# Routed slots of a two-layer kernel: who fetches a slot's rows and who turns them

## The reference

```
x  = x + attn0(xn) + ffn0(xn)        # chunked linear attention; 16 gated experts of width 128, all tokens
xn = layernorm(x)
x  = x + attn1(xn) + ffn1(xn)
attn1: top-2 of 4 gated linear scans  h_t = a_t*h_{t-1} + sigmoid(g)*tanh(v)
ffn1:  logits = xn @ gate_w.T + gate_b + expert_bias;  e = argmax(logits)     # one of 8 experts a token
       y = relu(xn @ w1[e] + b1[e]) @ w2[e] + b2[e]                           # 256 -> 1024 -> 256
```

## Time and profile before

| what | us |
|---|---|
| runs of the kernel before | 1044.45 median (1044.31 to 1044.87, 3 runs) |
| the profiled execution | 1045.66 |
| its span | 1043.9 |
| TensorE busy | 1032.9 (99% of the span) |
| VectorE busy | 769.4 (74%) |
| ScalarE busy | 629.2 (60%) |
| GpSimd busy | 318.4 (31%) |

### The profile page before, as it was taken

One profiled execution on the slowest core, in us unless ns is written; L12 is line 12 of the kernel. 1 busy time (PEld: TensorE's weight loads), 2 busy tenths in 40 slices (PEclk: granted clock), 3 DMA queues, 4 the chain that ended last, 5 costly groups with the idle time before them and its releaser, 6 DMA issues. The chain is left out here.

```text
span 1043.9 us, 19992 instructions
## 1 busy us (share of the span) xinstructions
PE 1032.9 (99%) x6566; PEld 921.3 (88%) x6566; DVE 769.4 (74%) x1247; ACT 629.2 (60%) x1186; POOL 318.4 (31%) x284
## 2 busy tenths in 40 slices
PE   8999999999999999999999999999999999999998
PEld 7988888889888888888877888999999999888887
DVE  6876667666666666767779998877777677588887
ACT  4654445444444454545566666788888888566665
POOL 3343343443434344343452782000000000372000
PEclk9999999999999999999999999999999999999999
DMA  6135213022131221623156275587887776552203
GB/s 195 60 97 202 82 41 100 6 79 55 40 100 40 80 60 41 217 67 142 42 202 262 82 268 205 183 269 266 275 273 252 266 253 212 210 170 90 84 17 102
DMA packets 108402, 148.46 MB, mean 142 GB/s; under 512 B 39616, under 2 KB 76352, under 8 KB 107328
## 3 DMA queue, kind: packets, MB, share of 16 engines
q1 hardware_dynamic: 99584, 133.80, 38.7%
q0 software_dynamic: 3072, 8.39, 2.4%
q10 hardware_dynamic: 5696, 5.64, 1.6%
HBM read 105.53 MB, written 42.27 MB: 142 GB/s over the span
## 5 line engine op out<-in xcount | busy, mean ns | idle before, releaser
L793 POOL TENSOR_TENSOR acc<-acc,ytmp 128x512 f32<-128x512 f32 x120 | 156.4, 1303 | 260.2 <-ACT ytmp L884 240.0
L1602 ACT ACTIVATE act_o<-ps,scan_bias 128x512 f32<-128x512 f32 x189 | 129.7, 688 | 100.0 <-PE ps L392 95.8
L884 ACT ACTIVATE ytmp<-ps,sel 128x256 f32<-128x256 f32 x256 | 107.3, 470 | 99.4 <-PE ps L1141 98.7
L961 DVE SCALAR_TENSOR_TENSOR hT_l<-ps,hT_h 128x512 fp32r<-128x512 f32 x128 | 87.8, 686 | 89.4 <-ACT hT_h L844 88.6
L1139 PE MATMUL ps<-vals_h,hT_h 128*128 128x256 f32 x512 | 145.3, 284 | 1.1 <-DVE hT_l L961 0.7
L1140 PE MATMUL ps<-vals_l,hT_h 128*128 128x256 f32 x512 | 143.6, 281 | 0.0
L1141 PE MATMUL ps<-vals_h,hT_l 128*128 128x256 f32 x512 | 143.5, 280 | 0.0
L844 ACT ACTIVATE hT_h<-ps 128x512 fp32r<-128x512 f32 x128 | 76.3, 596 | 96.5 <-PE ps L392 89.5
L1926 DVE TENSOR_TENSOR_SCAN h_b<-a_b,hstate,xs_b 128x512 f32<-128x512 f32 x63 | 88.2, 1400 | 30.3 <-ACT a_b L1609 26.8
L1754 POOL DMA_INDIRECT late_y<-y_d,pos_i x20 | 23.1, 1157 | 273.0 <-DMA y_d<-y_sb 267.2
L1139 PEld LDWEIGHTS ps<-vals_h,hT_h 128*128 128x128 f32 x512 | 96.3, 188 | 11.1 <-issue 4.6
(11 more groups left out here) (258 smaller groups left out, 2765.5 us busy)
## 6 DMA issues: line engine op xcount, KB each, us to landing
raw<-w SPq DMA_DIRECT2D x78, 512.0 KB, 4.3
x1T<-xT_d SPq DMA_DIRECT2D x16, 512.0 KB, 5.1
comb_b<-comb_d SPq DMA_DIRECT2D x8, 1024.0 KB, 8.3
xn_d<-xn SPq DMA_DIRECT2D x15, 512.0 KB, 2.9
w_small<-w SPq DMA_DIRECT2D x14, 512.0 KB, 4.3
xs_d<-zeros ACTq DMA_DIRECT2D x1, 4992.0 KB, 19.7
x_d<-x SPq DMA_DIRECT2D x8, 512.0 KB, 4.5
xT_d<-nT_h SPq DMA_DIRECT2D x8, 512.0 KB, 2.6
```

The costliest lines, as they stand in the source:

```text
L793: pool.tensor_tensor(dst[:, 2:4, :], acc[:, 2:4, :], ytmp[:, k % 2, :, :], ALU.add).then_inc(acc23, 1)
L884: act.activation(ytmp[:, k % 2, j - 2, :], yb(k, j), ACT.Copy, scale=sel[:, j, k:k + 1]).then_inc(y_23, 1)
L1602: act.activation(act_o[:, i % 2, w, :], ps[:, 3 * (i % 2) + w, :], func, bias=scan_bias[:, w, i:i + 1]).then_inc(act_g, 1)
```

## The change

- TensorE no longer turns rows. VectorE does it, with one transpose instruction per slot (`turn_rows`) that turns 32x32 squares. So that this gives the full transpose, the rows are laid out in SBUF in another way: partition quarter q holds columns 64q to 64q+63 of 32-row pieces, and the host permutes the rows of `w1` to match.
- The rows come in four transfers for a slot, one for each quarter, of 32 partitions and 256-byte runs, issued by GpSimd (`load_rows` on `pool`) once the transpose of the slot before them in the list is done (`turned`). Before it was one transfer on SyncE's queue, with 1 KB runs.
- In a plain slot VectorE turns the next rows after piece 0, ScalarE rounds them after piece 1 and VectorE makes their rest after piece 2. In a big slot VectorE turns after piece 2, and the other two stay at the end. `sT_small` is written by VectorE directly.
- In scan group 3 GpSimd makes the products of steps 4 to 7 and the sums of steps 6 and 7; both were VectorE's.
- SyncE loads the plain slot's weights at the end of its list for k = 0, behind the other weights.
- The rankings stand one behind each piece of slot 21; before, all stood at its end with `mixture_top`, which is now in slot 22.

The core of the diff:

```diff
-    rows = rc("rows", [P, ST, D], F32)
+    rows = rc("rows", [P, ST * P // Q32, DC * Q32], F32)
+    sT32 = rc("sT32", [P, DC, SLOT], F32)
-    xs_v = xs_d.rearrange("(b p) d -> b p d", p=P)
+    xs_q = xs_d.rearrange("(g r) (b k) -> b r g k", r=Q32, b=P // Q32)
...
+    def mixed_on_dve(g, i):
+        return isinstance(g, int) and g >= 2 and not (g == B_FIRST - 1 and i >= MC - DC)
+    def product_on_pool(g, i):
+        return zero(g) or (isinstance(g, int) and g == B_FIRST - 1 and i >= MC // 2)
...  SyncE, slot(r, k)
                 if left(r, k) > 1:
-                    load_rows(r, k + 2)
-                    if k == 0:
-                        load_w1_small(r, expert_at(r, ST))
...
                 if left(r, k) > 1:
                     raw2_half(n + 2, 0, expert_at(r, k + 2))
+                    if k == 0:
+                        load_w1_small(r, expert_at(r, ST))
...  TensorE
-            def rows_T(r, k):
-                pe.wait_ge(rows_in, 16 * (n + 1))
-                for c in range(DC):
-                    for i in range(st):
-                        last_mm = pe.transpose(ps[:, 6, (c * st + i) * P:(c * st + i + 1) * P],
-                                               rows[:, i, c * P:(c + 1) * P], ident[:])
-                if left(r, k) > 0:
-                    rows_T(r, k + 1)
...  ScalarE, slot(r, k)
                     relu(n, k, q, st * P)
                     round_e(n, q, st * P)
+                    if q == 1 and small(k):
+                        rows_hi(r, k + 1)
...
-                    rows_hi(r, k + 1)
+                    if not small(k) and not small(k + 1):
+                        rows_hi(r, k + 1)
...  GpSimd
+            def load_rows(r, k):
+                n = ROUND * r + k
+                if not zero(n):
+                    wait_alone(pool, turned, n)
+                b, st = blocks(r, k)
+                n_q = P // Q32
+                for q in range(n_q):
+                    quarter = slice(q * Q32, (q + 1) * Q32)
+                    pool.dma_start(rows[quarter, 0:st * n_q, :],
+                                   xs_q[q][:, bass.ds(b * n_q, st * n_q), :]).then_inc(rows_in, 16)
+            for g in range(B_FIRST - 1):
+                body(g)
+            all_scattered(pool)
+            load_rows(0, 0)
+            body(B_FIRST - 1)
+            every_slot(load_next, pool)
...  VectorE
+            def turn_rows(r, k):
+                n, (_, st) = ROUND * r + k, blocks(r, k)
+                dve.wait_ge(rows_in, 16 * (P // Q32) * (n + 1))
+                dst = sT_small if small(k) else sT32
+                if not small(k) and not zero(n):
+                    dve.wait_ge(sT_ok, bigs(r, k))
+                dve.transpose(dst[:].rearrange("p c (g r) -> p g c r", r=Q32),
+                              rows[:, 0:st * P // Q32, :].rearrange("p g (c a) -> p g c a", c=DC)).then_inc(turned, 1)
...  VectorE, slot(r, k)
                     low_e(n, q, st * P)
+                    if left(r, k) == 1:
+                        mixture_rank(dve, link, mix2, q)
+                    if q == (0 if small(k) else 2) and left(r, k) > 0:
+                        turn_rows(r, k + 1)
+                    if q == 2 and small(k):
+                        rows_lo(r, k + 1)
```

More of the change, by code:

```diff
@@ L51 @@
 CHUNK = 32
+Q32 = 32
 Q32 = 32
@@ L597, in build @@
     w1_hi, w1_lo, w2_hi, w2_lo = (sem(n) for n in ("w1_hi", "w1_lo", "w2_hi", "w2_lo"))
-    T_full, sT_hi, sT_ok = sem("T_full"), sem("sT_hi"), sem("sT_ok")
+    turned, sT_hi, sT_ok = sem("turned"), sem("sT_hi"), sem("sT_ok")
     l1_full, t_ok, e_hi, e_ok, l2_part, ys_ok, y_st = (
@@ L1344, in raw2_half @@
                              a["w2"][bass.ds(e, 1), h].rearrange("a p j d -> p (a j) d")).then_inc(r2_in[h], 16)
[L1346 to L1351, removed]
             def load_b1(n, k, e):
@@ L1528, in slot @@
                 W = st * P
-                pe.wait_ge(sT_ok, n + 1)
+                if small(k):
+                    pe.wait_ge(turned, n + 1)
+                else:
+                    pe.wait_ge(sT_ok, bigs(r, k) + 1)
                 for q in range(FJ // 2):
@@ L1626, in rows_hi @@
             def rows_hi(r, k):
[L1627 to L1633, removed]
+                act.wait_ge(turned, ROUND * r + k + 1)
+                act.activation(sT_h[:], sT32[:], ACT.Copy).then_inc(sT_hi, 1)
             def relu(n, k, q, W):
@@ L1716, in _, with xs @@
             pool.memset(within[:, :, 0:1], 0.0).then_inc(r_io, 1)
[L1718 to L1722, removed]
+            def xs(g, i):
+                n = MC * g + i
+                if n >= 2:
+                    pool.wait_ge(scan_ok, n - 1 if product_on_pool(g, i - 1) else n)
+                pool.wait_ge(act_g, 3 * n + 2)
                 pool.tensor_tensor(xs_b[:, i % 2, :], act_o[:, i % 2, 0, :], act_o[:, i % 2, 1, :],
@@ L1758, in body @@
                 if zero(g):
-                    xs(0)
+                    xs(g, 0)
                 for i in range(MC):
-                    if zero(g) and i + 1 < MC:
-                        xs(i + 1)
-                    if i >= DC and not mixed_on_dve(g):
+                    if i + 1 < MC and product_on_pool(g, i + 1):
+                        xs(g, i + 1)
+                    if i >= DC and not mixed_on_dve(g, i):
                         mix(g, i)
@@ L1768, in _, with load_next @@
             rstd(pool, mv1, stats1[:, :, 0], rstd1, mvs1, pe1, rs1, GROUPS - 1)
-            for g in range(B_FIRST):
+            def load_rows(r, k):
[8 more added lines that the diff above has]
+                                   xs_q[q][:, bass.ds(b * n_q, st * n_q), :]).then_inc(rows_in, 16)
+            def load_next(r, k):
+                if left(r, k) > 0:
+                    load_rows(r, k + 1)
+            for g in range(B_FIRST - 1):
                 body(g)
+            all_scattered(pool)
+            load_rows(0, 0)
+            body(B_FIRST - 1)
+            every_slot(load_next, pool)
             pool.wait_ge(y_st, 16 * NSLOT)
@@ L1912, in step @@
                     return
-                if not zero(g):
+                if not product_on_pool(g, i):
                     dve.wait_ge(act_g, 3 * n + 2)
@@ L1941, in step @@
                                   ALU.mult).then_inc(hw_ok, 1)
-                if i >= DC and mixed_on_dve(g) and not (final(g) and i >= MC - DC):
+                if i >= DC and mixed_on_dve(g, i) and not (final(g) and i >= MC - DC):
                     if i >= MC - DC:
@@ L2000, in rows_out @@
                                   ALU.add).then_inc(ys_ok, 1)
-            def mixture_pieces(slots_left):
-                if slots_left == 1:
-                    for j in range(M):
-                        mixture_rank(dve, link, mix2, j)
-                    mixture_top(dve, link, mix2)
-                else:
-                    mixture_finish(dve, link, mix2, 2)
             def slot(r, k):
@@ L2023, in slot @@
                 if left(r, k) > 0:
-                    if not small(k + 1):
+                    if not small(k) and not small(k + 1):
                         rows_lo(r, k + 1)
@@ L2028, in slot @@
                     w2_half(n + 1, 0)
-                if left(r, k) < 2:
-                    mixture_pieces(left(r, k))
+                if left(r, k) == 0:
+                    mixture_top(dve, link, mix2)
+                    mixture_finish(dve, link, mix2, 2)
             g = GROUPS - 1
@@ L2061, in _ @@
                         w1_half(0, (i - 4) // 2)
+                    if g == B_FIRST - 1 and i == MC - 4:
+                        turn_rows(0, 0)
                     if g == B_FIRST - 1 and i == MC - 3:
@@ L2098 @@
         "expert_bias": c(i["L1_ffn_expert_bias"]),
-        "w1": c(i["L1_ffn_w1"].reshape(E1, DC, P, 2, F1 // 2).transpose(0, 3, 2, 1, 4)),
+        "w1": c(i["L1_ffn_w1"].reshape(E1, P // Q32, DC, Q32, 2, F1 // 2).transpose(0, 4, 1, 3, 2, 5)
+                .reshape(E1, 2, P, DC, F1 // 2)),
         "b1": c(i["L1_ffn_b1"].reshape(E1, FJ, P).transpose(0, 2, 1)),
```

19 lines of the change are left out of this document (4 added, 15 removed).

## The result

| what | before | changed |
|---|---|---|
| runs, us | 1044.43 median (1044.31 to 1044.87, 4 runs) | 1066.42 median (1062.26 to 1069.15, 4 runs) |
| profiled execution, its span | 1045.66, 1043.9 | 1062.26, 1060.6 |
| routed slots, first matmul to last | 239.6 | 257.0 |

A forecast was written before the change was run, and what follows sets the result against it. TensorE, busy 99% of the span, was taken as the bound. Turning -7.9, slot 0 +0.15, slot 1 -1.3, last slots -0.85 and plain slots +7.0 gave -2.9 us: 1041.5 us, range 1038 to 1051.5.

The forecast's parts named there:

- The turning leaves TensorE: Routed slots: TensorE saves 0.43 us per big slot's rows and 0.21 per plain slot's, -7.9 us; VectorE's transposes hidden in big slots.
- The plain slots: Seven plain slots: the new order delays VectorE's pieces, so TensorE waits; 1.0 us each, +7.0 us.
- How long a fetch takes: GpSimd's four row transfers land in 5.1 us; shortest time available, behind a plain slot, is 6.2 us.
- Start-up: Slot 0: +0.15 us, its own turning included; slot 1: weights issued sooner remove a wait, -1.3 us.
- slot 22: Last slots: spreading the rankings over the pieces removes TensorE's wait in slot 22, -0.85 us.
- Late rows: Rival: GpSimd's plain transfers as slow as indirect ones, VectorE waits in plain slots; at 7.0 us, 7.5 more, 1049.0; chance 0.32.
- Plain slots for free: Rival: plain slots' pieces come in time, 7.0 us stay, 1034.5, or 1038 with half; chance 0.12.

The follow-up runs named there:

- the weights early: The changed kernel with SyncE loading the plain slot's weights where it did before, ahead of the next big slot's halves: 1050.48 us, ratio 1.0058.
- the idle matmuls: The changed kernel plus unread matmuls in plain slots: 8 each ahead of j = 4 and 6, 1073.33 us; 4 ahead of j = 4 only, 1059.18 us.
- combined version: C with plain slots in big-slot order, no GpSimd products or sums in group 3, plain slot's weights early except in the first round: 1043.39 us.
- the three built on it: The combined version with plain slots' transpose behind piece 1, 1043.05 us; with 8 idle matmuls in slot 0, 1044.09; with both, 1042.60.
- C: The changed kernel itself, with the whole change, against the kernel before: 1066.42 us median, ratio 1.0203.
- No help: C with GpSimd's products and sums in scan group 3 undone, so VectorE does that group alone: 1061.90 us, ratio 1.0156.

## Why the prediction was wrong, by its own steps

**The turning leaves TensorE: right.** Slots without a wait are 0.42 and 0.16 us shorter (forecast 0.43 and 0.21), and VectorE's transposes are hidden in the big ones, 11.45 us.

**The plain slots: right by themselves.** Forecast 7.4 with a wait of 0.6 at j = 4; with the weights early slots 8, 14 and 20 take 7.40 with a wait of 0.52. I took this order as given, and it alone ate the gain.

**How long a fetch takes: the step that failed.** 5.1 us to landing, against a window of 6.2, is right for the other places: 4.5 to 5.5, with a spacing of 0.57 to 0.61 us (I took 0.88) and the first issue 0.8 after the transpose (I took 0.1). But I had one duration for all places, and its last term, 2.4 us from the last issue to landing, was the best of GpSimd's indirect transfers; their median was 3.7 and their longest 8.1. The row loads of the kernel before, issued by SyncE in the same slots, would have warned me:

```profile
DMA to landing us min/median/max: 2.2/4.0/6.8
```

Behind a plain slot that term measured 4.1 to 6.3 us in the changed kernel. Under start-up I had credited the weights' move with 1.3 us in slot 1 and charged nothing for it anywhere else, though it puts 1 MB and then two big halves in front of the rows in six more rounds. That made 6.6 to 8.7 us of the fetch (6.2 to 7.9 to its last packet), just where time was short: about 10 us of waiting, and no step of the sum had it. Undoing the move gives 15 of the 22 us, what hangs on the waits included.

**The clock: no step at all.** Each wait was priced at its length and 0.1 for starting again. Behind the waits of four plain slots and of slot 0 the granted clock was 0.50 for some 3 us each: 8.5 us of slow distances outside slot 0 against 1.9 before. That it follows the standing still is shown by where it fell and by the idle matmuls; of its price, 2.7 us in slots without a wait and 0.9 in slot 0 are shown, the rest is counted and not tested.

**Start-up: slot 1 and slot 22 right (-1.56 and -0.77, own turning included), slot 0 wrong.** I forecast that the help frees VectorE 1.2 us earlier. It handed GpSimd six instructions of 0.69 and got back longer ones of its own. Slot 0 is +2.8 instead of +0.15: 0.9 is the help, 0.9 the lower clock, and 1.0 is there without both.

**The rivals.** Late rows had the place and the sign, but a wrong cause (GpSimd's issue as slow as an indirect one) and at 7 us a price of 7.5 us more: half, as the fetch took 7.9 on average and the clock was missing. What the Trainium skill (SBUF — State Buffer, "Who interferes with whom") says beside it, that copies on VectorE starve GpSimd's transfers and tensor_tensor does not, was tried here for tensor_tensor alone, and there the trace agrees: for slot 11 GpSimd issued from 771.61 on, VectorE split weights from 772.49 to 774.85, and the packets of the four transfers began at 772.87, 773.48, 774.08 and 774.68, as evenly as the issues. "Plain slots for free" was excluded by the order, and became true in five of the seven once it was changed: 6.45 to 6.62 us.

**What stays open.** Why the runs of C spread over 7 us, those before over 0.6. Each wait for a load is another length in each profile, which fits, but no run tells it apart. Why the clock falls behind one wait and not behind another as long.

## What to carry to other kernels

Before you move a load, look at what is asked for in the 10 us behind its new place, by any queue; a queue of its own did not help the rows while the DMA engines were 96% busy. Take a load's landing from a row with the same traffic around it, and the longest one where time is short. TensorE, 99% busy at full clock, lost more by a wait than the wait: count some matmuls after it at half speed. And work given to GpSimd was here not taken off VectorE: six instructions of 0.69 us went away, and the slot behind came out 0.9 us longer.

## What was not expected of the hardware

- A plain transfer of 32 partitions and 64 KB on GpSimd's queue takes 0.58 us to issue, less than half the distance of an indirect one; landing 1.9/2.7/6.3 us.
- The fourth transfer of the fetch for slot 17, the 72nd of its kind and the 104th with the scatters, starts 3.1 to 5.8 us after the third, in all ten profiles in which GpSimd fetches; the next largest distance inside a fetch is 1.19, always at the 51st, and most are 0.6. In the combined version and the three built on it, slot 17 is 0.6 to 1.5 us longer than its like, VectorE waiting for these rows in slot 16 or for the next ones in slot 17. The cause was not looked for.
- TensorE's clock fell to 0.50 behind waits of 0.64 and 0.88 us in slot 5 of C, and stayed full behind one of 2.03 us in slot 0 of "No help". It came back to full by itself after some 3 us of continuous matmuls at the lower level.
